# Moving two silu products to GpSimd and two tiles' moments to VectorE in the last stage of an RWKV block with a mixture of experts

## The chip, the cores and the metric

One Trainium2 chip, one of its cores. The metric is the device time of one launch in microseconds (us).

## The reference

The input x has 8 sequences of 512 tokens and 512 channels, in float32. Two residual sublayers follow each other, each with a layer norm behind it:

```python
x = layernorm(x + attn(x))        # RWKV: k, v, r projections of time-mixed x, a scan over the tokens, then Wo
x = layernorm(x + ffn(x))         # 8 experts of inner width 16, of which each token takes its best 2

logits = einsum('bth,eh->bte', x, router_w); weights = softmax(logits)
gate = weights * (1 for the 2 largest, else 0)
h = einsum('bth,eih->beti', x, down_w);  a = silu(h)
out = einsum('beth,bte->bth', einsum('beti,ehi->beth', a, up_w), gate)
```

## The kernel before

A tile is 128 tokens of 512 channels (256 KB); the 8 sequences have 4 tiles each, numbered 0 to 31. Each engine has its own instruction list, written out by hand and run strictly in order; semaphores tie the lists together. A main loop of 32 slots does the scans of one sequence and, between them, the projections of the next and the second sublayer of an earlier one. Behind the loop stands the tail, the subject here: tiles 20 to 23, 24 to 27 and 28 to 31 (in the code t5, t6 and t7 plus 0 to 3) are finished there. What it does for a tile, with the engine:

- TensorE projects with Wo (`project_high`, `project_low`, `project_rest`). VectorE adds the residual (`residual`). ScalarE computes the first norm's statistics (`spread`: a square with its sum, a logarithm, an exponential); for tiles 29 and 31 VectorE measures the moments (`moments`, two instructions) and `spread` has two instructions left. GpSimd normalises (`normalise`).
- TensorE transposes the tile (`turn`), ScalarE copies that to SBUF (`turned`), TensorE makes the experts' inner values and the router's scores (`hidden`), and ScalarE copies them (`hidden_copy`).
- The gating works on steps k, each a group of tiles: step 6 is tiles 24 to 27, step 7 tiles 28 and 29, step 8 tiles 30 and 31 (in the code LAST - 1, LAST and LAST + 1). ScalarE computes the sigmoid and the softmax's exponential (`ffn_in`), VectorE the gates (`gate_scores`, `gate_top`), and then the gated silu is two multiplications (`silu`): inner value by sigmoid, and that by the gate. TensorE transposes the result (`ffn_turn`), ScalarE copies it (`ffn_out`), and TensorE multiplies it by up_w (`ffn_up`).
- VectorE adds that to the tile (`residual2`). The last norm needs its second moment alone: ScalarE makes it (`spread2`), from a square with its sum, or for tiles listed in `MEASURED` from the moments that VectorE has measured (`moments2`: `bn_stats`, `bn_aggr`), where only a logarithm and an exponential are left for ScalarE. GpSimd scales the tile (`normalise2`); tiles 29 and 31 are scaled by VectorE (`finish`), behind all else that it does.
- SyncE stores the tiles in the order of their numbers, each store behind the wait for its own tile.

TensorE's list at the end of the tail sets much of the order:

```python
turn(t7 + 2); hidden(t7 + 1); ffn_up(t5 + 2)
turn(t7 + 3); hidden(t7 + 2); ffn_up(t5 + 3)
hidden(t7 + 3); ffn_up(t6); ffn_turn(LAST)
ffn_up(t6 + 1); ffn_up(t6 + 2)
ffn_turn(LAST + 1); ffn_up(t6 + 3)
for t in range(t7, NT * NB): ffn_up(t)
```

`ffn_turn(k)` waits until the k-th gated silu is done (semaphore agd), `ffn_up` of tiles 28 to 31 until `ffn_out` of its step. VectorE's `gate_scores(LAST + 1)` and ScalarE's `ffn_in(LAST + 1)` wait for the copy of tile 31's inner values (semaphore hc). The silu of steps 7 and 8 works in buffers M, EX and DEN, all in SBUF. GpSimd does the same two multiplications already for steps 0 to 5, on groups twice as large.

Of the kernel before, what the change touches and what calls it, by code (L numbers as in the profile page):

```python
# [12 lines left out]
NB, T, H = 8, 512, 512  # L13
C = H // 128
NT = T // 128
# [4 lines left out]
LAST = NB - 1  # L20
# [9 lines left out]
def rwkv_moe_postln(nc, x, xt, vec, wk, wv, wr, wo, dr, up, tri, out):  # L30
    with ExitStack() as ctx:
# [66 lines left out]
        def xn_at(t):  # L98
            b, n = divmod(t, NT)
            return XT[:, n, 1:T + 1] if b == LAST else XN[b % 2][:, n, :]  # L100

        def col(t):
            b, n = divmod(t, NT)
            i = NT * (2 if b == LAST else b % 2) + n
            return slice(i, i + 1)
# [54 lines left out]
        def up_at(t):  # L160
            if t // NT == LAST:
                return tail_bank(t, PT, PK[0], PK[1], PV)
            if t // NT == LAST - 1:
                return tail_bank(t, PV, PR, PP, PU)
            return tail_bank(t, PU, PT, PK[0], PU) if t // NT == LAST - 2 else PU[:, :]

        MEASURED = [NT * LAST + 1, NT * LAST + 2, NT * LAST + 3]

        MEASURED1 = [NT * LAST + 1, NT * LAST + 3]

# [5 lines left out]
        def squared(t, measured):  # L176
            return t + 1 - sum(m <= t for m in measured)
# [401 lines left out]
        def _(eng):  # L579
            eng.preload_act_table_set(TABLES)  # L580

            def act(s, *a, **k):
                eng.activation(*a, **k).then_inc(q[s], 1)  # L583
# [46 lines left out]
            def spread(t):  # L630
                if t in MEASURED1:
                    i = MEASURED1.index(t)
                    eng.wait_ge(q["mv1"], i + 1)
                    act("lv1", LV1[:, col(t)], MV[:, 5 + i, 1:2], ACT.Ln, bias=EPS)
                else:
                    eng.wait_ge(q["res"], t + 1)
                    act("sq1", JUNK[:, :], xn_at(t), ACT.Square, bias=SUM1[:, col(t)], scale=-float(H),
                        accum_out=SQ1[:, col(t)])
                    eng.wait_ge(q["sq1"], squared(t, MEASURED1))
                    act("lv1", LV1[:, col(t)], SQ1[:, col(t)], ACT.Ln, bias=EPS, scale=float(H) ** -3)  # L640
                eng.wait_ge(q["lv1"], t + 1)
                act("rs1", RS1[:, col(t)], LV1[:, col(t)], ACT.Exp, scale=-0.5)

            def spread2(t, n=1):
                cols = slice(col(t).start, col(t).start + n)
                if t in MEASURED:
                    i = MEASURED.index(t)
                    eng.wait_ge(q["mv2"], i + n)
                    eng.activation(LV2[:, cols], MV[:, i:i + n, 1], ACT.Ln, bias=EPS).then_inc(q["lv2"], n)
                else:  # L650
                    for u in range(t, t + n):
                        eng.wait_ge(q["res2"], u + 1)
                        act("sq2", JUNK[:, :] if u == t else KT[:, 0, :], xn_at(u), ACT.Square, accum_out=SQ2[:, col(u)])
                    eng.wait_ge(q["sq2"], squared(t + n - 1, MEASURED))
                    eng.activation(LV2[:, cols], SQ2[:, cols], ACT.Ln, bias=EPS, scale=1.0 / H).then_inc(q["lv2"], n)
                eng.wait_ge(q["lv2"], t + n)
                eng.activation(RS2[:, cols], LV2[:, cols], ACT.Exp, scale=-0.5).then_inc(q["rs2"], n)

            def turned(t):
                eng.wait_ge(q["tr"], t + 1)  # L660
                if t == NT * LAST:
                    eng.wait_ge(q["lo"], 3 * C * LAST)
                elif t == FIRST:
                    eng.wait_ge(q["wol"], 1)
                    eng.wait_ge(q["wol1"], 1)
                elif t and t < FIRST:
                    eng.wait_ge(q["h"], t)
                elif FIRST + 2 <= t < NT * LAST:
                    eng.wait_ge(q["h"], t - 1)
                act("x1t", x1t_at(t), turned_at(t).rearrange("p (c t) -> p c t", c=C), ACT.Copy)  # L670
# [14 lines left out]
            def hidden_copy(t):  # L685
                eng.wait_ge(q["h"], t + 1)
                act("hc", hs_at(t), hidden_at(t), ACT.Copy)
# [19 lines left out]
            def ffn_out(k):  # L707
                p = PARTS[k]
                eng.wait_ge(q["agt"], k + 1)
                if k < LAST - 1:  # L710
                    eng.wait_ge(q["up_"], NT * k)
                elif k == LAST - 1:
                    eng.wait_ge(q["rw"], U)
                act("agc", p.agt, p.turned_at, ACT.Copy)
# [98 lines left out]
            t5, t6, t7 = (NT * (LAST - i) for i in (2, 1, 0))  # L813
# [4 lines left out]
            turned(t7)  # L818
            spread(t7 + 2)
            ffn_out(LAST - 1)  # L820
            spread2(t5)
            turned(t7 + 1)
            hidden_copy(t7)
            spread(t7 + 3)
            turned(t7 + 2)
            hidden_copy(t7 + 1)
            ffn_in(LAST)
# [7 lines left out]
            ffn_out(LAST + 1)  # L835
            spread2(t5 + 3)
            spread2(t6, 2)
            spread2(t6 + 2, 2)
            for t in range(t7, NT * NB):
                spread2(t)  # L840

# [2 lines left out]
        def _(eng):  # L844
# [89 lines left out]
            def residual2(t):  # L934
                eng.wait_ge(q["up_"], t + 1)
                eng.tensor_tensor(xn_at(t), up_at(t), xn_at(t), ALU.add).then_inc(q["res2"], 1)
# [12 lines left out]
            def moments2(t):  # L949
                i = MEASURED.index(t)  # L950
                eng.wait_ge(q["res2"], t + 1)
                eng.bn_stats(ST[:, i, :], xn_at(t)).then_inc(q["st2"], 1)
                eng.wait_ge(q["st2"], i + 1)
                eng.bn_aggr(MV[:, i, :], ST[:, i, :]).then_inc(q["mv2"], 1)
# [53 lines left out]
            def silu(k):  # L1008
                p = PARTS[k]
                eng.wait_ge(q["sg"], k + 1)  # L1010
                eng.tensor_tensor(p.tiled(p.s1), p.tiled(p.s1), p.hs[:, :, 0:EI], ALU.mult).then_inc(q["sh"], 1)
                eng.wait_ge(q["sh"], k + 1)
                eng.wait_ge(q["gg"], k + 1)
                a, o = (s.rearrange("p (n i) -> p n i", i=I) for s in (p.s1, p.s2))
                eng.tensor_tensor(o, a, p.gs[2].unsqueeze(2).to_broadcast([128, p.n * E, I]), ALU.mult)\
                   .then_inc(q["agd"], 1)
# [99 lines left out]
            t5, t6, t7 = (NT * (LAST - i) for i in (2, 1, 0))  # L1116
# [11 lines left out]
            gate_scores(LAST)  # L1128
            residual2(t5 + 2)
            gate_top(LAST)  # L1130
            silu(LAST)
            residual2(t5 + 3)
            gate_scores(LAST + 1)
            gate_top(LAST + 1)
            silu(LAST + 1)
            for n in range(NT):
                residual2(t6 + n)
            residual2(t7)
            residual2(t7 + 1)
            moments2(t7 + 1)  # L1140
            residual2(t7 + 2)
# [8 lines left out]
        def _(eng):  # L1150
# [15 lines left out]
            def silu(k):  # L1166
                p = PARTS[k]
                eng.wait_ge(q["sg"], k + 1)
                eng.tensor_tensor(p.tiled(p.s1), p.tiled(p.s1), p.hs[:, :, 0:EI], ALU.mult).then_inc(q["sh"], 1)
                eng.wait_ge(q["sh"], k + 1)  # L1170
                eng.wait_ge(q["gg"], k + 1)
                a, o = (s.rearrange("p (n i) -> p n i", i=I) for s in (p.s1, p.s2))
                eng.tensor_tensor(o, a, p.gs[2].unsqueeze(2).to_broadcast([128, p.n * E, I]), ALU.mult)\
                   .then_inc(q["agd"], 1)
# [22 lines left out]
            def normalise(t):  # L1197
                i = MEASURED1.index(t) if t in MEASURED1 else None
                total, scale = (SUM1[:, col(t)], -1.0 / H) if i is None else (MV[:, 5 + i, 0:1], -1.0)
                eng.wait_ge(q["rs1"], t + 1)  # L1200
                eng.tensor_scalar(NM1[:, col(t)], total, RS1[:, col(t)], scale, ALU.mult, ALU.mult)\  # L1201
                   .then_inc(q["nm1"], 1)
                eng.wait_ge(q["nm1"], t + 1)
                eng.tensor_scalar(xn_at(t), xn_at(t), RS1[:, col(t)], NM1[:, col(t)], ALU.mult, ALU.add)\
                   .then_inc(q["nrp"], 1)

            def normalise2(t):
                eng.wait_ge(q["rs2"], t + 1)
                eng.tensor_scalar(xn_at(t), xn_at(t), RS2[:, col(t)], ZERO[:, :], ALU.mult, ALU.add)\
                   .then_inc(q["nrm2"], 1)  # L1210
# [83 lines left out]
            t5, t6, t7 = (NT * (LAST - i) for i in (2, 1, 0))  # L1294
            last_lows(3)
            for n in range(NT - 1):
                normalise(t7 + n)
            normalise2(t5)
            normalise(t7 + 3)
            for t in range(t5 + 1, NT * NB):  # L1300
                if t not in FINISHED:
                    normalise2(t)

# [32 lines left out]
```

## Time and profile before

| | |
|---|---|
| median of 3 runs | 462.37 us (462.35 to 462.37) |
| profiled execution, its own time | 462.28 us |
| its span, first to last instruction | 460.5 us |
| granted TensorE clock, mean | 0.996 of full speed |
| busy over the span | TensorE 97%, VectorE 88%, ScalarE 77%, GpSimd 68% |
| instructions | 6679 |

The span is what the trace's times count from 0 to 460.5. The profiled execution took 1.78 us more than its span. PE stands for TensorE, PEld for its weight loads, DVE for VectorE, ACT for ScalarE, POOL for GpSimd, SPq for SyncE's queue. ScalarE's instructions all have line 583, except the logarithm and the exponential of `spread2`. An instruction's duration can overlap that of the next one on its engine, since the engines are pipelined: the distance between two starts tells what an instruction costs in a row.

### The profile page before, as it was taken

The numbers are of one execution on the slowest core, as the hardware profiler recorded it, in microseconds if no ns is written. First come the engines' busy times: TensorE is split into PE (matmuls) and PEld (weight loads), VectorE is DVE, ScalarE is ACT, GpSimd is POOL, SyncE is SP. The second block draws the span as 40 slices with busy tenths as digits, with TensorE's granted clock in tenths as the row PEclk, the third lists the DMA queues.
The fourth block names the chain that finished last, engine by engine and source line by source line (L and its number), as shares of the span: only waits on it lengthen the run. The fifth ranks groups of instructions, "written<-read, shape, count | busy, mean of one in ns | idle before, by whom it ended". The sixth has DMA issues, their size and how long they took to land.

```text
span 460.5 us, 6679 instructions
## 1 busy us (share of the span) xinstructions
PE 445.7 (97%) x1984; PEld 340.3 (74%) x1984; DVE 405.3 (88%) x615; ACT 355.9 (77%) x801; POOL 312.2 (68%) x301
## 2 busy tenths in 40 slices
PE   8999998999999999999999999999999999999993
PEld 3444655777888888888888888888888888888761
DVE  5989979999788989999898998989898996975976
ACT  1666757778688789888788897888798887768695
POOL 2454777388668898579957697569965695754334
PEclk9999999999999999999999999999999999999998
DMA  8603220032000042100420043100430023400016
GB/s 247 212 0 118 91 91 1 1 111 96 1 1 0 1 157 83 36 0 28 157 93 0 1 137 93 46 0 24 139 107 7 1 69 93 137 1 0 0 48 228
DMA packets 20244, 30.64 MB, mean 67 GB/s; under 512 B 2032, under 2 KB 7152, under 8 KB 20208
## 3 DMA queue, kind: packets, MB, share of 16 engines
q1 hardware_dynamic: 20208, 30.21, 20.1%
q8 instruction: 16, 0.26, 0.2%
q14 instruction: 20, 0.16, 0.1%
HBM read 21.82 MB, written 8.39 MB: 66 GB/s over the span
## 4 chain that ended last, share of the span: by engine, by line
PE 73%; DVE 5%; ACT 2%; issue 1%; POOL 1%; POOLq 0%; DVEq 0%; ACTq 0%
PE PH L442 5%; PE PV L325 5%; PE PV L329 5%; PE PV L326 5%; PE PK L325 5%; PE PR L325 5%; PE PK L329 5%; PE PR L329 5%; PE PK L326 5%; PE PR L326 5%; PE PP L352 4%; PE PP L353 4%; PE PP L357 4%; PE PT L424 3%; PE PP L372 1%
## 5 line engine op out<-in xcount | busy, mean ns | idle before, releaser
L583 ACT ACTIVATE PR<-PR 128x512 f32<-128x512 f32 x128 | 74.6, 583 | 33.2 <-DVE PR L891 12.6
L1195 POOL TENSOR_TENSOR DQ<-DEN,EX 128x512 f32<-128x512 f32 x32 | 41.3, 1289 | 20.5 <-DVE DEN L862 20.5
L1201 POOL TENSOR_SCALAR NM<-SUM,RS 128x1 f32<-128x1 f32 x30 | 8.0, 266 | 64.3 <-ACT RS L583 64.3
L916 DVE SCALAR_TENSOR_TENSOR KT<-D,VEC,XT 128x512 f32<-128x512 f32 x57 | 48.2, 892 | 0.0
L325 PE MATMUL PK<-KH,WKH 128*128 128x512 f32 x112 | 46.2, 413 | 0.6 <-DVE NUM L879 0.6
L325 PE MATMUL PV<-VH,WVH 128*128 128x512 f32 x112 | 45.9, 410 | 0.0
L325 PE MATMUL PR<-RH,WRH 128*128 128x512 f32 x112 | 44.5, 398 | 0.2 <-DVE RW L903 0.2
L329 PE MATMUL PR<-RL,WRH 128*128 128x512 f32 x112 | 44.2, 394 | 0.6 <-POOL RL L1163 0.6
L329 PE MATMUL PV<-VL,WVH 128*128 128x512 f32 x112 | 43.9, 392 | 0.0
L329 PE MATMUL PK<-KL,WKH 128*128 128x512 f32 x112 | 43.9, 392 | 0.0
L326 PE MATMUL PK<-KH,WKL 128*128 128x512 f32 x112 | 43.8, 391 | 0.0
L326 PE MATMUL PV<-VH,WVL 128*128 128x512 f32 x112 | 43.7, 391 | 0.0
L326 PE MATMUL PR<-RH,WRL 128*128 128x512 f32 x112 | 43.7, 390 | 0.0
L1163 POOL TENSOR_TENSOR RL<-D,RH 128x512 fp32r<-128x512 f32 x28 | 40.3, 1467 | 4.6 <-ACT RH L583 4.6
L862 DVE TENSOR_TENSOR_SCAN DEN<-PK,EX 128x512 f32<-128x512 f32 x32 | 38.9, 1217 | 2.3 <-ACT PK L583 1.6
L583 ACT ACTIVATE EX<-PK 128x512 f32<-128x512 f32 x32 | 19.1, 598 | 28.1 <-DVE PK L855 28.1
L583 ACT ACTIVATE EX<-EX 128x512 f32<-128x512 f32 (+1 forms) x66 | 40.4, 612 | 0.1
L879 DVE TENSOR_TENSOR_SCAN NUM<-PK,EX 128x512 f32<-128x512 f32 x32 | 39.2, 1225 | 1.1
L1163 POOL TENSOR_TENSOR VL<-KT,VH 128x512 fp32r<-128x512 f32 x28 | 38.3, 1389 | 1.8 <-ACT VH L583 1.8
L849 DVE TENSOR_TENSOR_SCAN M<-CST,PK 128x512 f32<-128x512 f32 x32 | 38.8, 1211 | 0.1
L583 ACT ACTIVATE PK<-PK 128x512 f32<-128x512 f32 x64 | 38.4, 600 | 0.0
L1163 POOL TENSOR_TENSOR KL<-KT,KH 128x512 fp32r<-128x512 f32 x28 | 35.4, 1292 | 2.6 <-ACT KH L583 2.6
(274 smaller groups left out, 1284.8 us busy)
## 6 DMA issues: line engine op xcount, KB each, us to landing
XT<-in_xt SPq DMA_DIRECT2D x32, 256.0 KB, 3.3
XN<-in_x SPq DMA_DIRECT2D x28, 256.0 KB, 2.6
out<-XN SPq DMA_DIRECT2D x28, 256.0 KB, 2.0
X1T<-in_wo SPq DMA_DIRECT2D x1, 1024.0 KB, 5.2
XT<-in_x SPq DMA_DIRECT2D x4, 256.0 KB, 4.0
out<-XT SPq DMA_DIRECT2D x4, 256.0 KB, 2.4
X1T<-in_wk SPq DMA_DIRECT2D x2, 256.0 KB, 4.9
XN<-in_wv SPq DMA_DIRECT2D x2, 256.0 KB, 5.6
```

The lines of the kernel that those rows point to most:

```text
L325: eng.matmul(dst[:, :], wh[:, c, o], high[:, c, :], start=(c == 0), stop=False)
L326: eng.matmul(dst[:, :], wl[:, c, o], high[:, c, :], start=False, stop=False)
L329: last = eng.matmul(dst[:, :], wh[:, c, o], low[:, c, :], start=False, stop=(c == C - 1))
L352: eng.matmul(projected_at(t), high(c), WOH[:, c, :], start=(c == 0), stop=False)
L442: last = eng.matmul(hidden_at(t), x1t_at(t)[:, c, :], DR[:, c, :], start=(c == 0), stop=(c == C - 1))
L583: eng.activation(*a, **k).then_inc(q[s], 1)
L849: eng.tensor_tensor_scan(M[:, 1:T + 1], TD[:, j:j + 1].to_broadcast([128, T]), PK[u % 2][:, :], NEG, ALU.add, ALU.max).then_inc(q["m"], 1)
L862: eng.tensor_tensor_scan(DEN[:, 1:T + 1], PK[u % 2][:, :], EX[:, 0, :], 0.0, ALU.mult, ALU.add)\
L879: eng.tensor_tensor_scan(NUM[:, 1:T + 1], PK[u % 2][:, :], EX[:, 0, :], 0.0, ALU.mult, ALU.add)\
L916: eng.scalar_tensor_tensor(out=full(b, which, c), in0=D[:, c, :], scalar=VEC[:, 2 + which, c:c + 1], in1=XT[:, c, 0:T], op0=ALU.mult, op1= ...
L1163: eng.tensor_tensor(lo[:, c, :], full(b, which, c), hi[:, c, :].bitcast(F32), ALU.subtract)\
L1195: eng.tensor_tensor(DQ[:, :], DEN[:, 0:T], EX[:, 1, :], ALU.add).then_inc(q["e"], 1)
```

## The change

Three edits in the tail, and one list that follows from them.

- `silu` of steps 7 and 8 leaves VectorE's list and enters GpSimd's: the first behind `normalise2` of tile 20, the second behind `normalise2` of tile 21. GpSimd's `normalise` of tile 31 now stands ahead of `normalise2` of tile 20.
- VectorE measures the moments of tiles 27 and 28 too, both behind the `residual2` of tile 28 and ahead of that of tile 29. ScalarE's `spread2` takes tiles 26 and 27 one by one, 26 with a square, 27 and 28 from the moments.
- ScalarE's `spread` of tile 31 (the last first norm's statistics) changes places with `spread2` of tile 20: it stands directly behind `ffn_out` of step 6, and `spread2` of tile 20 behind `hidden_copy` of tile 28.

```diff
-        MEASURED = [NT * LAST + 1, NT * LAST + 2, NT * LAST + 3]
+        MEASURED = [NT * LAST - 1, NT * LAST, NT * LAST + 1, NT * LAST + 2, NT * LAST + 3]
...
             ffn_out(LAST - 1)
-            spread2(t5)
+            spread(t7 + 3)
             turned(t7 + 1)
             hidden_copy(t7)
-            spread(t7 + 3)
+            spread2(t5)
             turned(t7 + 2)
...
             spread2(t6, 2)
-            spread2(t6 + 2, 2)
+            spread2(t6 + 2)
+            spread2(t6 + 3)
             for t in range(t7, NT * NB):
                 spread2(t)
...
             gate_top(LAST)
-            silu(LAST)
             residual2(t5 + 3)
             gate_scores(LAST + 1)
             gate_top(LAST + 1)
-            silu(LAST + 1)
             for n in range(NT):
                 residual2(t6 + n)
             residual2(t7)
+            moments2(t6 + 3)
+            moments2(t7)
             residual2(t7 + 1)
...
             for n in range(NT - 1):
                 normalise(t7 + n)
+            normalise(t7 + 3)
             normalise2(t5)
-            normalise(t7 + 3)
-            for t in range(t5 + 1, NT * NB):
+            silu(LAST)
+            normalise2(t5 + 1)
+            silu(LAST + 1)
+            for t in range(t5 + 2, NT * NB):
                 if t not in FINISHED:
                     normalise2(t)
```

## Rows read from the trace of the kernel before

**Rows 1.** One stretch: us busy of PE, PEld, DVE, ACT, POOL; clock, DMA share, GB/s

```profile
451.00:455.00 4.00, 1.71 (x4) 0.40 (x3) 3.80 (x8) 3.54 (x17) 2.87 (x4) 1.00 0.53 197
```

**Rows 2.** The chain that ended last, 447 to 457: start us, us, what

```profile
447.50 0.43 DVE DEN L1015
...
447.98 0.44 PE PH L461 x2
448.42 0.86 PE PU L494 x2
...
451.03 0.70 DVE XT L936
451.76 0.71 DVE ST L952
```

**Rows 3.** Timeline of VectorE: start us, us, engine, line, operation, tiles

```profile
437.62 0.18 DVE L943 BATCH_NORM_AGGREGATE MV<-ST 128x2 f32<-128x6 f32 x1
...
447.84 0.68 DVE L936 TENSOR_TENSOR XN<-PV,XN 128x512 f32<-128x512 f32 x1
448.44 0.68 DVE L936 TENSOR_TENSOR XN<-PR,XN 128x512 f32<-128x512 f32 x1
...
452.49 0.18 DVE L954 BATCH_NORM_AGGREGATE MV<-ST 128x2 f32<-128x6 f32 x1
452.59 0.66 DVE L936 TENSOR_TENSOR XT<-PK,XT 128x512 f32<-128x512 f32 x1
...
455.63 1.47 DVE L947 TENSOR_SCALAR XT<-XT,RS 128x512 f32<-128x512 f32 x2
```

**Rows 4.** Timeline of ScalarE

```profile
438.86 0.58 ACT L583 ACTIVATE D<-PV 128x512 f32<-128x512 f32 x1
...
442.84 0.58 ACT L583 ACTIVATE D<-PV 128x512 f32<-128x512 f32 x1
...
444.76 0.28 ACT L583 ACTIVATE EX<-PP 128x136 f32<-128x136 f32 x1
...
445.71 1.30 ACT L583 ACTIVATE M<-M 128x256 f32<-128x256 f32 x3
...
452.25 0.61 ACT L583 ACTIVATE KT<-XN 128x512 f32<-128x512 f32 x1
```

**Rows 5.** Timeline of TensorE

```profile
439.58 1.17 PE L442 MATMUL PP<-DR,D 128*128 128x136 f32 x8
...
443.56 1.17 PE L442 MATMUL PP<-DR,D 128*128 128x136 f32 x8
...
446.50 1.02 PE L494 MATMUL PP<-KT,NU 128*128 128x512 f32 x2
...
448.25 1.02 PE L494 MATMUL PU<-KT,NU 128*128 128x512 f32 x2
```

**Rows 6.** GpSimd's groups, shapes apart: count, busy us, mean ns, idle before

```profile
L1173 POOL TENSOR_TENSOR X1T<-X1T,GS 128x512 f32<-128x512 f32 x6 | 6.4, 1062 | 20.6 <-DVE GS L1000 20.6
...
L1244 POOL TENSOR_TENSOR WOL<-X1T,WOH 128x1024 fp32r<-128x1024 f32 x1 | 2.4, 2367 | 0.0
```

**Rows 7.** GpSimd's line 1169 alone (ns min/median/max), and its timeline at 433 us

```profile
L1169 POOL TENSOR_TENSOR X1T<-X1T,HS x6: 1278/1744/1762, 131.9 to 400.0; 128x512 f32<-128x512 f32 x6
...
433.58 0.26 POOL L1201 TENSOR_SCALAR NM<-SUM,RS 128x1 f32<-128x1 f32 x1 [3.88 <-ACT RS L583]
433.95 0.77 POOL L1204 TENSOR_SCALAR XT<-XT,RS,NM 128x512 f32<-128x512 f32 x1
```

**Rows 8.** Lines 947 and 1209 in the tail: ns min/median/max, first and last start

```profile
L947 DVE TENSOR_SCALAR XT<-XT,RS x2: 558/721/884, 455.6 to 456.2; 128x512 f32<-128x512 f32 x2
...
L1209 POOL TENSOR_SCALAR XT<-XT,RS,ZERO x2: 770/851/932, 455.1 to 455.9; 128x512 f32<-128x512 f32 x2
```

**Rows 9.** The last four stores (line 246): ns of an issue; first and last start; landing

```profile
L246 SPq DMA_DIRECT2D out<-XT x4: 333/429/451, 455.9 to 457.3; - x4
...
DMA to landing us min/median/max: 2.0/2.0/2.7
```

## The prediction

> **What bounds the kernel now.** I read the page for the whole, then the table of stretches, the chain in order of time, and each engine's timeline from 437 us on. TensorE is busy 97% of the span, but the edits lie in the tail, so the average does not answer. In the stretches the reader is to see that the bound has changed hands by 451: of the 4 us from there TensorE fills 1.71, VectorE 3.80, ScalarE 3.54 [rows 1]. The chain names the places. It runs over VectorE's second silu product of step 8 (447.50, 0.43 long), over TensorE's transposes of that (447.98) and `ffn_up` of tiles 27, 28 and 29, and comes back to VectorE at 451.03 with `residual2` of tile 29; from there VectorE's own residuals and moments follow without a gap [rows 2]. After them come tile 31's statistics on ScalarE, `finish` of tiles 29 and 31 (455.63 to 457.10), and the last store [rows 3, 9]. So two waits decide: when step 8's silu is ready for TensorE, and how much VectorE has to do between tile 28 and the end.
>
> **Early statistics.** `spread` of tile 31 needs VectorE's moments, which are there at 437.80 [rows 3], about when it would now start. Ahead of `turned` of tile 29 a square of some 0.6 goes and short instructions stay, so this copy, at 438.86 before, starts that much earlier [rows 4]. TensorE's `hidden` of tile 29 started at 439.58, 0.14 behind the copy's end at 439.44 [rows 4, 5]. It can't take the 0.6, because the transposes of tile 30 stand ahead of it on TensorE, and these don't wait for the copy. The gain is between nothing and the 0.14 by which `hidden` trailed the copy; `hidden` of tile 31 (443.56) stood just as far behind its copy (443.42) [rows 4, 5], so a release takes about that long, and the transposes had been done just about then. I take 0.12; the difference to either end is smaller than all else here. GpSimd's `normalise` of tile 31 comes earlier too, but TensorE reaches the transposes that want it no sooner than by this 0.12. The 0.12 passes down: the inner values of step 7, ScalarE's `ffn_in`, `turned` and `hidden` of tile 31, its own copy at 444.64 in place of 444.76, and the sigmoid of step 8, which ended at 445.71 + 1.30 = 447.01 and now ends at 446.89 [rows 4, 5]. Gain 0.12.
>
> **Step 7's silu.** VectorE is relieved of two products (some 0.8 us). But behind them it does one residual and then waits for the copy of tile 31's inner values, which ended at 445.04 and will end at 444.92 [rows 4]. The 0.8 turns into idle time: gain 0. On GpSimd the products take about 1.5 us (below) and are ready near 444.5; TensorE wants them behind `ffn_up` of tile 24, at 445.3. If that cover of 0.8 were gone, the excess would be on TensorE's list in full. `normalise2` of tile 21 follows at about 444.6, as before.
>
> **Step 8's silu.** VectorE had both products done at 447.93, 0.92 behind the sigmoid's end at 447.01 [rows 2, 4]; on its list they cost 0.80 (they start as the sigmoid ends, and tile 24's residual follows at 447.84 [rows 3]). The trace has no product of 128x256 on GpSimd. The same two at 128x512 take 1.28 at the least and 1.74 in the median, and 1.06 [rows 6, 7]. Half of that, as if nothing in it were fixed, is 0.64 and 0.53: the lower bound. A difference of 128x1024 takes 2.37 [rows 6], so twice the width costs 1.09 more than 1.28, hence 0.19 of it is fixed and 128x256 would take 0.74 and 0.63; with the slow case of the first (half of 1.74, 0.87) the upper bound is 0.87 and 0.63. I take 0.70 and 0.58, between the free rows, since no product with two SBUF inputs is left on VectorE then that could slow them. Between two dependent instructions GpSimd needs 0.11 (433.84 to 433.95) [rows 7]; I take the same from ScalarE to it, and 0.05 from it to TensorE, as VectorE had [rows 2]. The transposes start at 446.89 + 0.11 + 0.70 + 0.11 + 0.58 + 0.05 = 448.44 (bounds 448.33 to 448.60), against 447.98: TensorE loses 0.46. It has nothing to do meanwhile: `ffn_up` of tile 26 started at 446.50 [rows 5] and a pair of such matmuls takes 0.86 in a row [rows 2], so 0.12 earlier it is free at 447.24 and waits 1.2 us. Behind the waiting instruction stand `ffn_up` of tiles 27 to 31, all that VectorE still needs from it.
>
> The Trainium skill's GPSIMD Engine Reference, section 3.1, says that GpSimd needs about 2.6 cycles for an element of a two-input operation, and measured 4497 ns at 2048 elements, nearly twice VectorE's time. An estimate by that page alone is 0.56 us for each product, which would put the transposes at 448.28. The wider row of this trace (2.37 at 1024) agrees with such a slope.
>
> **VectorE between tiles 26 and 29.** Without the products it starts `residual2` of tile 24 at about 446.92 (447.84 less 0.80 and 0.12) [rows 3]. With a pitch of 0.60 [rows 3] tiles 24, 25 and 26 go by 448.7, but tile 27 needs `ffn_up`: 0.27 behind the transposes' start [rows 2, 5], 448.71, and 1.02 long, so 449.73. Tile 28's is 0.86 behind, 450.59, and its residual starts at 450.63. The time won is lost here again. Then the two new moments: from one `bn_stats` to its aggregate is 0.73 (451.76 to 452.49), and the next starts 0.10 later (452.59) [rows 2, 3], so 0.83 each, 1.66 for both. They stand ahead of tile 29's residual. Only 0.26 of a wait would have been there to hide them in (tile 29's `ffn_up` is 0.86 behind tile 28's, a residual takes 0.60). So tile 29's residual starts at 450.63 + 0.60 + 1.66 = 452.89, against 451.03 [rows 2]: +1.86. From there to the last aggregate VectorE had no gap and its list is unchanged: all of it moves by 1.86.
>
> **ScalarE and GpSimd behind that.** ScalarE loses a square for tile 27 and one for tile 28 and gains one pair of short instructions: two times 0.61 [rows 4] less that, about 1.0 us less. It had no long wait there, but its results for tiles 24 to 28 only feed GpSimd and early stores. Gain for the end: 0.
>
> **The last microseconds.** `finish` of tile 31 took 0.88, that of tile 29 only 0.56; over the former lay GpSimd's last `normalise2` (0.93 where its neighbour took 0.77) [rows 8]. After the change that one (tile 30) is done at about 457.4, and `finish` of tile 31 starts at about 458.07, alone: I take 0.56, ending at 457.10 + 1.86 - 0.33 = 458.63, +1.53. Stores: that of tile 29 can go at 455.63 + 1.86 + 0.56 + 0.04 = 458.09; an issue takes 0.43 in the median [rows 9], so that of tile 31 goes two issues later, at 458.95, against 457.3 before: +1.65. From there to landing was 2.7, where a lone store needs 2.0 [rows 9]; the burst at the end shrinks from four stores to three, since tile 28 leaves earlier. I take 2.5, 0.2 less. Sum: 1.65 - 0.20 = +1.45.
>
> The Trainium skill (SBUF, State Buffer, section "Who interferes with whom") has VectorE and GpSimd share one pair of ports, which the first to start holds for its whole instruction; `tensor_scalar` on VectorE can be of the kind that takes it. By that rule the 0.33 comes back, as taken; if the row's 0.88 stayed, the end of `finish` would be 458.96 and the last store, queued behind two issues, would hardly move. The trace agrees with the rule by the pair 0.56 and 0.88.
>
> **The sum.** 460.5 + 1.45 + 1.78 outside the span is 463.7 for a profiled execution of 462.28; the median lies 0.09 above that, so 463.8 us.
>
> **Rivals.**
> - *The moments fall into waits, or GpSimd is quick.* If GpSimd delivered before TensorE is free (447.24), tile 28's residual would start 0.60 behind tile 27's, at 449.3, and VectorE's own work would count: two moments (1.66) for two products (0.80), less the 0.12, is +0.7 at tile 29, less 0.33 and 0.2, so +0.2: 462.6, no change by measurement. It needs both products in 0.15 us together; what it has in its favour is that each smaller error (GpSimd at its lower bound -0.1, landing at 2.0 -0.5) leads towards it: both together give +0.8, 463.2. I can't tell changes within 0.2% (0.92 us) from none.
> - *GpSimd is slower than any row suggests*, each product over 1 us (a fixed share I don't see, or waits for the port). Each 0.1 us on it is 0.1 on the end: with 1.0 and 1.0 it would be +0.7 more, 464.5. Step 7's cover of 0.8 would nearly be used up as well.
> - *ScalarE and GpSimd set the end, not VectorE.* For: ScalarE is nearly full to 455, and GpSimd's last `normalise2` ended at 455.9 + 0.93 = 456.8 [rows 8], right ahead of the last two issues of stores. If that chain decided, 1.0 us less on ScalarE would bring it forward in full: 461.3, faster. The point is whether the last `normalise2` waits for its queue or for tile 30's moments. Against: `finish` of tile 31 stands behind all of VectorE's moments, which grow in number, and the last store waits for it.
>
> **How the numbers follow.** The forecast 0.66 (its own range 463.1 to 464.3); GpSimd much slower 0.06; little or no change 0.22; faster 0.06. Some of the forecast's own range lies under the 0.92 bound (463.3), and I keep that in the chances: slower 0.69, same 0.25, faster 0.06. The bounds of the unknown costs (GpSimd -0.1 to +0.2, landing -0.5 to +0.2, pitch of the stores -0.2) give 462.9 to 464.3; reaching into both neighbours, the range is 462.6 to 464.5.
>
> **What the profile after would show.** `hidden` of tile 29 and the sigmoid of step 8 some 0.12 earlier; VectorE idle some 0.8 ahead of `gate_scores` of step 8; GpSimd's two products of 0.64 to 0.87 and 0.53 to 0.63; a wait of TensorE of 1.2 us ahead of the transposes of step 8; two more `bn_stats` between the residuals of tiles 28 and 29, and the latter near 452.9; `finish` of tile 31 at 0.56. I am wrong if TensorE's whole list moves forward by much more than 0.12, if GpSimd is not what the transposes wait for, or if the last store doesn't follow `finish` of tile 31.

## The result, and the profile after

The changed kernel takes 463.58 us (median of 10 runs, 463.24 to 463.91), the kernel before 462.49 (10 runs, 462.35 to 462.65): the ratio is 1.0024, with an interval of 1.0014 to 1.0034. That is 1.1 us slower, where +1.45 was forecast. The forecast time of 463.8 is only 0.2 off, but part of that is luck: it started from a median of 462.37 for the kernel before, which was 462.49 here.

The profiled execution of the changed kernel took 463.91, and its span is 462.1 against 460.5. The difference of 1.6 is more than the 1.1 of the medians, and TensorE's timeline shows why. The first row is the transposes of tile 29, which stand in the tail ahead of everything that the change touches; behind it are `hidden` of tiles 29 and 31 and the transposes of step 8's silu:

```profile
437.35 0.63 PE L424 MATMUL PV<-IDN,XT 128*128 128x128 f32 x4 [0.87 <-POOL XT L1205]
...
439.88 1.09 PE L442 MATMUL PP<-DR,D 128*128 128x136 f32 x8
...
443.79 1.17 PE L442 MATMUL PP<-DR,D 128*128 128x136 f32 x8
...
448.80 0.44 PE L461 MATMUL PH<-IDN,DEN 128*128 128x128 f32 x2 [1.05 <-POOL DEN L1174]
```

They started at 436.90 in the profile before, so this execution came into the tail 0.45 late. In the profiles of the ten experiments below the same instruction starts anywhere from 436.67 to 438.28, and single runs of the kernel before spread from 462.05 to 463.86. So I count the tail from that start and call it T. From T to the end the kernel before needs 23.60 us, the changed one 24.75: +1.15, which fits the medians. Each kernel has one profile, but counted from T they agree closely where their lists are alike: the transposes of step 8 stand at 11.45 or 11.46 in the four kernels that share the lists ahead of them. The end is coarser, since the span is given to 0.1.

The chain that ended last (start, us, what) now goes over GpSimd:

```profile
446.82 0.42 ACT M L583
447.24 0.07 issue
447.31 0.74 POOL M L1170
448.05 0.07 issue
448.12 0.63 POOL DEN L1174
448.75 0.04 issue
448.80 0.44 PE PH L461 x2
449.23 0.86 PE PU L494 x2
450.09 0.87 PE PT L494 x2
450.97 0.02 issue
450.99 0.69 DVE XT L937
```

From the sigmoid's end (447.24) to the transposes (448.80) are 1.56 us; before it was 447.01 to 447.98, 0.97 [rows 2, 4]. TensorE, free since 447.59 (446.73 for `ffn_up` of tile 26, and 0.86 in a row), stands idle for it, and VectorE's timeline shows the next engine to wait:

```profile
448.44 0.68 DVE L937 TENSOR_TENSOR XN<-PP,XN 128x512 f32<-128x512 f32 x1
450.13 0.69 DVE L937 TENSOR_TENSOR XN<-PU,XN 128x512 f32<-128x512 f32 x1 [1.01 <-PE PU L494]
450.99 0.69 DVE L937 TENSOR_TENSOR XT<-PT,XT 128x512 f32<-128x512 f32 x1 [0.17 <-PE PT L494]
451.60 0.68 DVE L953 BATCH_NORM_STATS2 ST<-XN 128x6 f32<-128x512 f32 x1
452.32 0.18 DVE L955 BATCH_NORM_AGGREGATE MV<-ST 128x2 f32<-128x6 f32 x1
452.42 0.66 DVE L953 BATCH_NORM_STATS2 ST<-XT 128x6 f32<-128x512 f32 x1
453.11 0.18 DVE L955 BATCH_NORM_AGGREGATE MV<-ST 128x2 f32<-128x6 f32 x1
453.21 0.66 DVE L937 TENSOR_TENSOR XT<-PK,XT 128x512 f32<-128x512 f32 x1
```

VectorE waits 1.01 ahead of tile 27's residual, and right behind that wait it does 1.61 us of new moments, ahead of tile 29's. That is the change in one view: idle time, and then added work behind it. The last scaling (line 948: ns min/median/max, first and last start) and the last stores:

```profile
L948 DVE TENSOR_SCALAR XT<-XT,RS x2: 457/472/486, 457.8 to 458.4; 128x512 f32<-128x512 f32 x2
L246 SPq DMA_DIRECT2D out<-XT x4: 332/382/447, 456.4 to 459.1; - x4
DMA to landing us min/median/max: 2.0/2.0/2.5
```

It takes 0.49 in place of 0.88, since GpSimd's last `normalise2` was over before [rows 8]; the last store lands 2.5 behind its issue and not 2.7 [rows 9].

The row of GpSimd's last `normalise2` (tile 30) shows that it ended at 457.67, ahead of both scalings, and ScalarE's row for tile 31 that it waits for VectorE's moments:

```profile
456.90 0.77 POOL L1210 TENSOR_SCALAR XT<-XT,RS,ZERO 128x512 f32<-128x512 f32 x1 [0.49 <-ACT RS L657]
457.89 0.20 ACT L649 ACTIVATE LV<-MV 128x1 f32<-128x1 f32 x1 [1.08 <-DVE MV L955]
```

### The profile page after: what moved, and what is told of

Same layout as the page of the kernel before. It is cut to its first block, busy times and chain, and to the rows that moved or that the text cites. A ratio compares the mean times of both kernels' runs of the same rounds, so it can differ in the third digit from the quotient of the medians.

```text
span 462.1 us, 6679 instructions
## 1 busy us (share of the span) xinstructions
PE 445.1 (96%) x1984; PEld 340.2 (74%) x1984; DVE 405.0 (88%) x615; ACT 355.2 (77%) x799; POOL 314.6 (68%) x305
## 4 chain that ended last, share of the span: by engine, by line
PE 73%; DVE 4%; ACT 2%; POOL 1%; issue 1%; POOLq 0%; DVEq 0%; ACTq 0%
PE PH L442 5%; PE PV L325 5%; PE PV L329 5%; PE PV L326 5%; PE PK L325 5%; PE PR L325 5%; PE PK L329 5%; PE PR L329 5%; PE PK L326 5%; PE PR L326 5%; PE PP L352 4%; PE PP L353 4%; PE PP L357 4%; PE PT L424 3%; PE PP L372 1%
```

## The experiments

All were timed against the kernel before on the same chip, 11 or 12 runs each. "From T" is taken from the profile; the ratio comes from the runs, and is not exactly the quotient of the two medians.

**Step 8's silu alone on GpSimd.**

```diff
             gate_top(LAST + 1)
-            silu(LAST + 1)          # VectorE
...
-            for t in range(t5 + 1, NT * NB):
+            normalise2(t5 + 1)      # GpSimd
+            silu(LAST + 1)
+            for t in range(t5 + 2, NT * NB):
```

> The kernel before with one part: step 8's silu alone goes to GpSimd. Theory A (two losses, one of them TensorE's wait): the two products end some 0.6 us later behind the sigmoid than on VectorE, TensorE waits about 1.1 us ahead of the transposes of step 8, and all that follows moves by that: +0.5 to +0.6 us, with VectorE idle by about 1 us between tiles 26 and 27. Rival B (only VectorE's amount of work counts): VectorE has 0.8 us less to do, so -0.5 to 0 us. Rival C (the loss comes from ahead of the tail, where the changed kernel's profile has tile 29's transposes 0.45 us later): then no part of the change in the tail costs much, and this one shows 0 to +0.2.

463.09 against 462.70, ratio 1.0012 (1.0003 to 1.0020): +0.4 us by the medians, about +0.55 by the ratio; from T to the end 24.26, +0.66. The transposes of step 8 start 11.68 behind T in place of 11.08, and tile 29's residual is as late:

```profile
448.82 0.44 PE L461 MATMUL PH<-IDN,DEN 128*128 128x128 f32 x2 [1.05 <-POOL DEN L1172]
```

```profile
450.15 0.69 DVE L936 TENSOR_TENSOR XN<-PU,XN 128x512 f32<-128x512 f32 x1 [1.01 <-PE PU L494]
451.01 0.69 DVE L936 TENSOR_TENSOR XT<-PT,XT 128x512 f32<-128x512 f32 x1 [0.17 <-PE PT L494]
451.87 0.69 DVE L936 TENSOR_TENSOR XT<-PK,XT 128x512 f32<-128x512 f32 x1 [0.17 <-PE PK L494]
```

The three residuals stand 0.86 apart, TensorE's pitch: VectorE, with 0.8 us less to do, only follows it. Rival B falls, theory A holds.

**Step 7's silu alone on GpSimd.** Since step 8's stays on VectorE, it got semaphores of its own.

```diff
             gate_top(LAST)
-            silu(LAST)              # VectorE
...
             normalise2(t5)          # GpSimd
             normalise(t7 + 3)
+            silu(LAST)
```

> The kernel before with one part: step 7's silu alone goes to GpSimd; step 8's stays on VectorE (with semaphores of its own). Theory A: the 0.8 us won on VectorE turn into a wait for tile 31's inner values, and GpSimd's products are done before TensorE wants them: -0.1 to +0.1 us. Rival B (only VectorE's amount of work counts): -0.8 us.

462.49 against 462.43, ratio 1.0000 (0.9991 to 1.0009); from T 23.58, -0.02. The 0.8 us taken from VectorE are worth nothing, as expected by theory A.

**The moments of tiles 27 and 28 alone.**

```diff
-        MEASURED = [NT * LAST + 1, NT * LAST + 2, NT * LAST + 3]
+        MEASURED = [NT * LAST - 1, NT * LAST, NT * LAST + 1, NT * LAST + 2, NT * LAST + 3]
...
             residual2(t7)
+            moments2(t6 + 3)
+            moments2(t7)
             residual2(t7 + 1)
```

> The kernel before with one part: VectorE measures the moments of tiles 27 and 28, both silus stay on VectorE. Theory A: tile 29's residual starts 1.4 to 1.5 us later (1.66 less what VectorE waited), 0.3 to 0.4 comes back because VectorE's last scaling no longer lies beside one of GpSimd's (0.49 to 0.56 long in place of 0.88), 0.2 more at the landing of the last store: +0.8 to +1.0 us. Rival D (the last stores' transfer sets the end, and earlier stores of tiles 27 and 28 relieve it): +0.3 or less. Rival C (loss from ahead of the tail): 0 to +0.3.

463.37 against 462.70, ratio 1.0015 (1.0007 to 1.0024), about +0.7; from T 24.41, +0.81, which is the lower edge of what was expected. Rivals C and D fall: T is at 436.79, and the loss is far above their 0.3. Tile 29's residual is 1.41 later, the last scaling takes 0.49 and the last store lands after 2.5: 0.6 of the 1.41 comes back behind it.

**The early statistics alone.**

```diff
             ffn_out(LAST - 1)
-            spread2(t5)
+            spread(t7 + 3)
             turned(t7 + 1)
             hidden_copy(t7)
-            spread(t7 + 3)
+            spread2(t5)
...
-            normalise2(t5)          # GpSimd
             normalise(t7 + 3)
+            normalise2(t5)
```

> The kernel before with one part: tile 31's first statistics move up on ScalarE, and its normalisation on GpSimd. Theory A: hidden of tile 29 is no longer held by the copy ahead of it, and the tail from there moves by 0.12 to 0.25 us: -0.1 to -0.25 us. Rival C (loss from ahead of the tail, set off by the changed order): +0.3 to +0.5 with tile 29's transposes late by as much as in the changed kernel.

462.27 against 462.70, ratio 0.9992 (0.9984 to 1.0001), an interval that touches 1. The profile decides more finely: `hidden` of tile 31 and the transposes of step 8 both start 0.22 nearer to T (6.44 for 6.66, 10.86 for 11.08), and the end is at 23.43, -0.17. Nothing is late ahead of T (436.67), so rival C falls.

**The changed kernel without the two moments.**

```diff
 # the changed kernel
-            moments2(t6 + 3)
-            moments2(t7)
```

with `MEASURED` and `spread2` as before.

> The changed kernel without the moments of tiles 27 and 28 on VectorE: both silus on GpSimd, early statistics. Theory A: early statistics -0.22, step 8's silu +0.60, so +0.3 to +0.45 us against the kernel before; VectorE's last scaling again lies beside GpSimd's and takes 0.9. Rival B (only VectorE's amount of work counts): -0.5 us or less.

462.91 against 462.43, ratio 1.0011 (1.0002 to 1.0020); from T 23.93, +0.33. The transposes of step 8 are at 11.46 (+0.38, which is 0.60 less 0.22), and the last scaling lies beside GpSimd's again and takes 0.89. Rival B falls here too.

**The changed kernel with step 8's silu back on VectorE.**

```diff
 # the changed kernel
             gate_top(LAST + 1)
+            silu(LAST + 1)          # VectorE, with the semaphores of its own
...
-            normalise2(t5 + 1)      # GpSimd
-            silu(LAST + 1)
-            for t in range(t5 + 2, NT * NB):
+            for t in range(t5 + 1, NT * NB):
```

> The changed kernel with step 8's silu back on VectorE. Theory A: transposes of step 8 at -0.22, the moments +1.41 at tile 29's residual, 0.6 of it back at the last scaling and the landing: +0.5 to +0.7 us against the kernel before. Rival E (the moments cost as much as VectorE has to do in all, and the silu's 0.8 more adds to it): +1.3 us or more, slower than the changed kernel.

463.06 against 462.43, ratio 1.0013 (1.0005 to 1.0022), about +0.6; from T 24.25, +0.65. VectorE has 0.8 us more to do than in the changed kernel, and the end is 0.5 nearer to T. Rival E falls.

**The same number of moments, in TensorE's wait.** The changed kernel, with tiles 25 and 26 measured in place of 27 and 28. VectorE does exactly as much as there; ScalarE's `spread2` takes tiles 24 to 27 one by one.

```diff
-        MEASURED = [NT * LAST - 1, NT * LAST, NT * LAST + 1, NT * LAST + 2, NT * LAST + 3]
+        MEASURED = [NT * LAST - 3, NT * LAST - 2, NT * LAST + 1, NT * LAST + 2, NT * LAST + 3]
...
-            for n in range(NT):
+            for n in range(NT - 1):
                 residual2(t6 + n)
-            residual2(t7)
-            moments2(t6 + 3)
-            moments2(t7)
+            moments2(t6 + 1)
+            moments2(t6 + 2)
+            residual2(t6 + 3)
+            residual2(t7)
```

> The changed kernel with the same amount of work on VectorE in another place: the moments of tiles 25 and 26 in place of 27 and 28, between the residuals of tiles 26 and 27, where VectorE waits 1.0 us for TensorE. Theory A (moments cost only what no wait covers): residual of tile 27 is 0.6 late, of 28 some 0.35, of 29 about 0.1, so the end is that of the kernel without the moments, +0.1 at most, or up to 0.4 less since the last scaling is alone: +0.1 to +0.5 us against the kernel before. Rival B (only VectorE's amount of work counts): as the changed kernel, +1.1 us.

462.39 against 462.43, ratio 0.9998 (0.9989 to 1.0007); from T 23.41, -0.19. VectorE's timeline:

```profile
448.10 0.68 DVE L936 TENSOR_TENSOR XN<-PP,XN 128x512 f32<-128x512 f32 x1
448.69 0.68 DVE L952 BATCH_NORM_STATS2 ST<-XN 128x6 f32<-128x512 f32 x1
449.41 0.18 DVE L954 BATCH_NORM_AGGREGATE MV<-ST 128x2 f32<-128x6 f32 x1
449.51 0.66 DVE L952 BATCH_NORM_STATS2 ST<-XN 128x6 f32<-128x512 f32 x1
450.20 0.18 DVE L954 BATCH_NORM_AGGREGATE MV<-ST 128x2 f32<-128x6 f32 x1
450.30 0.66 DVE L936 TENSOR_TENSOR XN<-PU,XN 128x512 f32<-128x512 f32 x1
450.88 0.68 DVE L936 TENSOR_TENSOR XT<-PT,XT 128x512 f32<-128x512 f32 x1
451.50 0.69 DVE L936 TENSOR_TENSOR XT<-PK,XT 128x512 f32<-128x512 f32 x1
```

There is no wait left in it, and tile 29's residual starts at 14.51 behind T (451.50 less 436.99), exactly as in the kernel without the two moments. 1.6 us of work cost nothing here, and the same 1.6 us cost the changed kernel 1.35 at that residual (15.86 less 14.51). Rival B, that only the amount of VectorE's work counts, falls altogether.

The result lies below the range that I had expected (+0.1 to +0.5). Against the kernel without the two moments the end even comes 0.5 nearer to T, with 1.6 us more work on VectorE: the last scaling takes 0.49 in place of 0.89, since GpSimd's last `normalise2` is over before, and the last store lands after 2.5 and not 2.7.

**Two versions built around step 8's silu on VectorE.** Both have the early statistics, step 7's silu on GpSimd, and tile 22's moments on VectorE ahead of `gate_scores` of step 8. The second also gives tile 29's square to ScalarE.

```diff
+        MEASURED = [NT * LAST - 6, NT * LAST + 1, NT * LAST + 2, NT * LAST + 3]   # the first
+        MEASURED = [NT * LAST - 6, NT * LAST + 2, NT * LAST + 3]                  # the second
...
             residual2(t5 + 3)
+            moments2(t5 + 2)
             gate_scores(LAST + 1)
...
-            moments2(t7 + 1)        # the second only
```

> Early statistics, step 7's silu on GpSimd, step 8's on VectorE, and one moment (tile 22) on VectorE ahead of gate_scores of step 8, where VectorE waits some 0.6 us. Theory A (the losses of the change are step 8's wait and the place of the moments; its early statistics are a gain of 0.2): -0.1 to -0.4 us against the kernel before. Rival B (VectorE's amount of work counts, which is as before): 0.

> As the kernel with tile 22's moment, and tile 29's moment goes from VectorE to ScalarE (a square), so that VectorE has 0.9 us less to do behind tile 29's residual. Theory A (VectorE's list behind that residual sets the end, while ScalarE has room): -0.5 to -0.9 us against the kernel before, less what a crowded drain of the last stores takes back. Rival F (the drain of the last stores sets the end): no faster than the kernel with tile 22's moment alone.

The first: 462.31 against 462.38, ratio 1.0000 (0.9991 to 1.0009), from T 23.52, -0.08, just short of the -0.1 to -0.4 expected. The moments overran their wait: the transposes of step 8 are at 10.98, 0.12 behind those of the early statistics alone. The second: 462.45 against 462.38, ratio 0.9999 (0.9990 to 1.0008), from T 23.53. I had expected it 0.5 to 0.9 faster and got nothing. Its timelines of VectorE and ScalarE at the end:

```profile
455.03 0.18 DVE L954 BATCH_NORM_AGGREGATE MV<-ST 128x2 f32<-128x6 f32 x1
455.90 0.49 DVE L947 TENSOR_SCALAR XT<-XT,RS 128x512 f32<-128x512 f32 x1 [0.70 <-ACT RS L657]
456.56 0.79 DVE L947 TENSOR_SCALAR XT<-XT,RS 128x512 f32<-128x512 f32 x1 [0.16 <-ACT RS L657]
```

```profile
455.67 0.20 ACT L657 ACTIVATE RS<-LV 128x1 f32<-128x1 f32 x1
455.78 0.19 ACT L649 ACTIVATE LV<-MV 128x1 f32<-128x1 f32 x1
456.00 0.20 ACT L657 ACTIVATE RS<-LV 128x1 f32<-128x1 f32 x1
456.11 0.19 ACT L649 ACTIVATE LV<-MV 128x1 f32<-128x1 f32 x1
456.32 0.20 ACT L657 ACTIVATE RS<-LV 128x1 f32<-128x1 f32 x1
```

VectorE's last aggregate is at 17.86 behind T, where the kernel before has it at 18.63, but ScalarE is only then through with its squares, and VectorE waits 0.70 and 0.16 for it. The bound has gone to ScalarE; rival F forecast the number, but the rows show another cause than the drain: the end of the last scaling, ahead of the last store, is no earlier than in the first version (20.18 and 20.12).

**Moments in the wait, and tile 29 on ScalarE.** The version with tiles 25 and 26 measured, and:

```diff
-        MEASURED = [NT * LAST - 3, NT * LAST - 2, NT * LAST + 1, NT * LAST + 2, NT * LAST + 3]
+        MEASURED = [NT * LAST - 3, NT * LAST - 2, NT * LAST + 2, NT * LAST + 3]
...
-            moments2(t7 + 1)
```

> The kernel with the moments of tiles 25 and 26 in TensorE's wait, and tile 29's moment goes from VectorE to ScalarE (a square). Theory A: against the kernel before -0.3 to -0.7 us. Rival F (the drain of the last stores sets the end): -0.1 to +0.1, as with tile 29 on VectorE.

461.76 against 462.38, ratio 0.9986 (0.9977 to 0.9995), 0.6 us faster than the kernel before; from T 22.89, -0.71. By its ratio this is 0.4% below the changed kernel, though the two were not timed side by side. ScalarE was given room by the two tiles whose moments VectorE takes in its wait, and uses it for tile 29's square: VectorE's wait of 0.70 ahead of the first scaling is gone, the one of 0.16 stays. Of the 0.71, 0.36 is there at the end of the last scaling; the rest lies behind it, in an earlier last issue (by 0.1 more) and a landing after 2.5 in place of 2.7. From T, in us:

```
                                 step 8's     tile 29's  end of the     end    ratio
                                 transposes   residual   last scaling
before                           11.08        14.13      20.20          23.60
changed kernel                   11.45        15.86      21.49          24.75  1.0024
step 8's silu alone              11.68        14.73      20.82          24.26  1.0012
step 7's silu alone              11.10        14.15      20.22          23.58  1.0000
moments alone                    11.08        15.54      21.17          24.41  1.0015
early statistics alone           10.86        13.91      19.99          23.43  0.9992
changed, without moments         11.46        14.51      20.58          23.93  1.0011
changed, step 8's silu back      10.86        15.32      20.95          24.25  1.0013
changed, moments in the wait     11.46        14.51      20.18          23.41  0.9998
tile 22 measured                 10.98        14.04      20.12          23.52  1.0000
tile 22 measured, 29 on ScalarE  10.97        14.02      20.18          23.53  0.9999
in the wait, 29 on ScalarE       11.46        14.51      19.84          22.89  0.9986
```

The four parts alone add up to +1.28 at the end, and the whole is +1.15.

## Why the prediction was right

The direction, the two places of the loss and their order came as forecast; the size was 0.3 to 0.4 us too high. By the steps:

- **Early statistics.** Forecast 0.12, measured 0.22, in the part alone and in the whole. `hidden` of tile 29 came nearer to T by 0.15, about the upper end of my bound: it starts 0.44 behind the start of tile 30's transposes now and 0.58 before. The rest comes inside it: its eight matmuls took 1.17 before and 1.09 now, so that `ffn_up` of tile 22 is already 0.23 nearer to T. I had let all behind `hidden` follow by the same amount only; why the matmuls became shorter was not followed up.
- **Step 7's silu.** Forecast 0, measured -0.02 alone. GpSimd's second product waited for the gates, which the first had held up (below), but ended at 444.98 and TensorE wanted it at 445.65: a cover of 0.7, where I had 0.8. VectorE's idle time ahead of `gate_scores` of step 8 is 0.49, where I had some 0.8: another 0.3 went into the instruction that was held up.
- **Step 8's silu.** The products took 0.73 and 0.62, inside the bounds and almost as the wider row had it (0.74 and 0.63); the forecast was 0.70 and 0.58. From the sigmoid to the transposes were 1.56 against 1.55 forecast, and that this fits so well is luck: the products took 0.08 more than forecast, and the three handovers between the engines 0.07 less (about 0.20 in place of 0.27). And the part alone moves the transposes by 0.60. With the early statistics' 0.22 off that, TensorE loses 0.37 and not 0.46. (The upper bound of the transposes adds up to 448.66, not 448.60, and the rival of a quick GpSimd needs both products in 0.08, not 0.15; neither changes the forecast.)
- **The moments.** 1.61 between tile 28's residual and 29's (1.66 forecast); tile 29's residual +1.73 from T (+1.86 forecast). The placement is what costs them: the same number of moments two residuals earlier, ahead of that of tile 27, costs nothing.
- **The last microseconds.** The last scaling took 0.49, not 0.56, so 0.40 came back where 0.33 was forecast. The end of `finish` moved by 1.29 (forecast 1.53), the last issue by about 1.35 (forecast 1.65), and the landing by -0.2, as forecast: +1.15 in all against +1.45.

The term that was mis-sized most is thus the first, by 0.10; 0.05 more stands in the moments, 0.07 in the last scaling, 0.06 between it and the last issue, and the remainder in small gaps.

None of the rivals was what happened. GpSimd was not quick: TensorE waits 1.05 for it. It was not slow either, with 0.73 and 0.62. And ScalarE doesn't set the end: it waits 1.08 for tile 31's moments. The rival of little or no change was the nearest; its argument, that time comes back at the last scaling (0.40) and at the landing (0.2), holds and stands in the forecast's own sum.

The rule of the Trainium skill (SBUF, State Buffer, "Who interferes with whom"), that the first of the two engines to start holds the shared ports, agrees with the runs. The last scaling took 0.88 to 0.91 in six kernels and 0.79 and 0.78 in the two with tile 29 on ScalarE; in all eight GpSimd's last `normalise2` had started first and lay over its start, and in all eight the scaling ended 0.28 behind GpSimd's instruction, whenever it had started. In the other four, the changed kernel among them, `normalise2` was over before and the scaling took 0.49. The estimate of 0.56 for a product, by the Trainium skill's GPSIMD Engine Reference (section 3.1), was too low: 0.73 and 0.62 were measured, and this trace's own wider rows were the better guide.

What stays open: the executions reach T at different times, 436.67 to 438.28, with no part of the changes ahead of it. Where in the main loop that arises was not followed up; it sets how finely a time can tell such changes apart.

## What to carry to other kernels

Work taken from an engine helps only as far as the next thing on its list is ready, and work given to it costs only what no wait covers. Here 0.8 us less ahead of a wait was worth 0, and 1.6 us more delayed the next residual by 1.35 behind a wait (and the end by 0.8) and by 0 inside it; so look in the trace for where an engine waits before choosing which work to move, and put the added work there. Where a slower engine takes over an instruction that another engine's in-order list waits for, its extra time lands on that list, less what the list has to do meanwhile: 0.6 in full for step 8, nothing for step 7, which had a cover of 0.7. When changes of a few tenths of a microsecond are compared by profiles, count from an instruction that the change can't touch.

## What the runs showed of the hardware

A product on GpSimd can hold up a tiny instruction of VectorE. In the changed kernel GpSimd's first product of step 7 (443.24, in its timeline) lies over three instructions of VectorE, of which the last is a product of 128x16 with both inputs in SBUF (443.56, in VectorE's):

```profile
443.24 0.74 POOL L1170 TENSOR_TENSOR M<-M,EX 128x256 f32<-128x256 f32 x1 [1.90 <-ACT M L583]
444.36 0.62 POOL L1174 TENSOR_TENSOR DEN<-M,EX 128x256 f32<-128x256 f32 x1 [0.39 <-DVE EX L1001]
```

```profile
443.24 0.16 DVE L993 RECIPROCAL EX<-EX 128x2 f32<-128x2 f32 x1
443.36 0.29 DVE L995 TENSOR_REDUCE EX<-NUM 128x16 f32<-128x128 f32 x1
443.56 0.45 DVE L997 TENSOR_TENSOR EX<-EX 128x16 f32<-128x16 f32 x1
444.04 0.17 DVE L1001 SCALAR_TENSOR_TENSOR EX<-EX 128x16 f32<-128x16 f32 x1
```

That product took 0.45, and ended 0.03 behind the end of GpSimd's at 443.98, where the same instruction of step 8, with GpSimd idle, took 0.16. The two with one input, ahead of it, took 0.16 and 0.29, where the kernel before has 0.15 and 0.29. It is so in all eight kernels with step 7's silu on GpSimd (0.43 to 0.45), and in none of the four others (0.17). GpSimd's second product then waited 0.39 for the gates that this made late: the engine that was to relieve the other had held it up, and paid for it itself. Beside residuals that read one operand from PSUM, GpSimd's products of step 8 ran at 0.73 and 0.62, and the residuals at 0.68, as without them.
